# Last units, expert layer and linear attention: another order of the tensor engine and seven rotating banks

## The reference

```python
attn = jax.nn.softmax(jnp.einsum('bgnc,bgckn->bgnk', qf, ks_), axis=-1)
out = jnp.einsum('bgnk,bgckn->bgnc', attn, vs_)          # layer 1: the value sums
...
router_probs = jax.nn.softmax(x @ router_w + router_b, axis=-1)
top_p, top_i = jax.lax.top_k(router_probs, K)
top_p = top_p / jnp.sum(top_p, axis=-1, keepdims=True)
expert_out = jnp.einsum('bnd,edc->bnec', x, expert_w) + expert_b
gathered = jnp.take_along_axis(expert_out, top_i[..., None], axis=2)
return jnp.einsum('bnk,bnkc->bnc', top_p, gathered)      # layer 4: the experts
...
q = (x @ wq_w.T + wq_b).reshape(b, s, h, d)              # layer 5: k and v likewise
q = jax.nn.elu(q) + 1.0
k = jax.nn.elu(k) + 1.0
kv_cos = jnp.einsum('bshx,bshz->bhxz', k_cos, v)
qkv = jnp.einsum('bshx,bhxz->bshz', q_cos, kv_cos) + jnp.einsum('bshx,bhxz->bshz', q_sin, kv_sin)
denom = 1.0 / (... + 1e-05)
```

## Time and profile before

| | us |
|---|---|
| median of 3 runs | 216.42 (215.61 to 217.93) |
| profiled execution | 216.58 |
| its span, first to last instruction | 214.8 |

### The profile page before, as it was taken

One profiled execution on the slowest core, in us unless ns is written; L12 is line 12 of the kernel. 1 busy time (PEld: TensorE's weight loads), 2 busy tenths in 40 slices (PEclk: granted clock), 3 DMA queues, 4 the chain that ended last, 5 costly groups with the idle time before them and its releaser, 6 DMA issues.

```text
span 214.8 us, 6817 instructions
## 1 busy us (share of the span) xinstructions
PE 186.6 (87%) x2969; PEld 136.4 (64%) x2969; DVE 154.1 (72%) x347; ACT 97.3 (45%) x239; POOL 39.2 (18%) x57
## 2 busy tenths in 40 slices
PE   7999989899997989974898798598499969979994
PEld 2677668899997889721344684244147737735993
DVE  2789997958999999869777166595768749646101
ACT  3734997478888778511003350200868510035100
POOL 4970000012421440540100301133000000110000
PEclk9999999999999999999699999969955999999999
DMA  6830426345455510000143140001200190000000
GB/s 180 285 117 5 154 95 201 107 133 197 150 158 166 180 49 3 4 0 5 22 159 99 27 110 0 0 5 32 67 25 3 25 366 22 0 0 0 3 0 24
DMA packets 9042, 17.07 MB, mean 79 GB/s; under 512 B 2504, under 2 KB 3752, under 8 KB 8884
## 3 DMA queue, kind: packets, MB, share of 16 engines
q1 hardware_dynamic: 8868, 16.34, 24.1%
q10 hardware_dynamic: 144, 0.30, 0.4%
HBM read 16.20 MB, written 0.42 MB: 77 GB/s over the span
## 4 chain that ended last, share of the span: by engine, by line
PE 57%; DVE 26%; issue 6%; ACT 5%; POOL 2%; DMA 2%; POOLq 1%; DVEq 0%
PE ps L1540 55%; DVE onehot L1068 5%; POOL rstd L578 2%; DVE dots L1094 2%; DMA cst<-in_cst 2%; DVE arena L453 2%; DVE att L1118 1%; ACT arena L641 1%; DVE stu_fq L1443 1%; ACT onehot L837 1%; ACT table L641 1%; ACT arena L858 1%; DVE dots L1100 1%; DVE arena L1524 1%; DVE arena L1048 1%
## 5 line engine op out<-in xcount | busy, mean ns | idle before, releaser
L1540 PE MATMUL ps<-table,onehot 128*128 128x64 bf16 x1728 | 52.9, 194 | 5.0 <-issue 2.8
L1540 PEld LDWEIGHTS ps<-table,onehot 128*128 128x128 bf16 x1728 | 51.5, 98 | 6.5 <-issue 4.8
L1540 PE MATMUL ps<-spare 128*128 128x512 bf16 (+1 forms) x128 | 36.6, 419 | 8.1 <-DVE rexp L1359 2.3
L725 ACT ACTIVATE arena<-ps 128x512 f32<-128x512 f32 (+1 forms) x40 | 21.5, 553 | 14.2 <-PE ps L1540 13.9
L1540 PEld LDWEIGHTS ps<-spare 128*128 128x128 bf16 x128 | 12.4, 109 | 24.4 <-issue 6.8
L453 POOL TENSOR_TENSOR arena<-arena,w4p 128x288 f32<-128x288 f32 x21 | 16.2, 803 | 57.9 <-DVE arena L453 57.8
L1540 PE MATMUL ps<-arena 128*32 128x66 f32 (+4 forms) x388 | 25.2, 281 | 0.2 <-DVE arena L1320 0.2
L1540 PEld LDWEIGHTS ps<-arena 128*32 128x32 f32 (+2 forms) x388 | 22.2, 156 | 4.1 <-issue 1.4
L578 POOL TENSOR_TENSOR rstd<-var_eps,cst 128x4 f32<-128x4 f32 (+2 forms) x9 | 8.8, 982 | 82.7 <-DVE var_eps L937 56.1
L641 ACT ACTIVATE arena<-ps 128x512 f32<-128x512 f32 (+3 forms) x16 | 7.0, 469 | 26.1 <-PE ps L1540 20.3
L1068 DVE TENSOR_SCALAR onehot<-indexb,cst 128x2304 bf16<-128x2304 bf16 (+1 forms) x24 | 17.7, 771 | 0.0
(11 more groups left out here) (280 smaller groups left out, 305.0 us busy)
## 6 DMA issues: line engine op xcount, KB each, us to landing
indexb<-index_rows SPq DMA_DIRECT2D x20, 288.0 KB, 3.3
stu_fq<-index_rows SPq DMA_DIRECT2D x8, 288.0 KB, 3.4
arena<-in_toep SPq DMA_DIRECT2D x1, 2120.5 KB, 9.6
l<-in_l SPq DMA_DIRECT2D x1, 646.5 KB
stu_fq<-in_stu SPq DMA_DIRECT2D x1, 560.0 KB, 3.8
onehot<-in_l3w SPq DMA_DIRECT2D x1, 512.0 KB
table<-stu_mixed SPq DMA_DIRECT2D x4, 128.0 KB, 2.2
l<-in_l SPq DMA_DIRECT2D x1, 384.0 KB, 7.3
```

The source lines that it names most:

```text
L725: nc.scalar.activation(gv[:, b % 2, :, at:at + count, :], ps[:, SB[n % len(SB)], 0:count * SLOT].rearrange("p (s a d) -> p a s d", s=count ...
L1540: return nc.tensor.matmul(out_ap, lhsT, rhs, start=start, stop=stop)
```

## The change

1. The sum over corners of unit 6 (`L - 1`) moves from VectorE to TensorE, like that of unit 5; the two have banks of their own. On VectorE the sum of unit 5 comes later, behind the logits of unit 7. The six spares around "linear middle" and "linear low" go; "linear low" and two spares now stand between the two transpositions of the heads.
2. Two spares instead of four in the attention.
3. In the expert layer five spares instead of eight behind the moments; the first half's expert products are ahead of the second half's transposition; the four spares behind the weighing go.
4. Linear attention: keys and values rotate over seven banks (2t mod 7, 2t + 1 mod 7), bank 7 is for transpositions and spares. The second half's transposition stands ahead of the first value products; from value tile 3 on, each step waits for one `vs`, and issues a value tile, the next key tile and a spare. Queries, key-value products and denominators take other banks.

The diff, cut; the lines that only rename banks on the reading engines are left out:

```diff
-        KBANK, VBANK = (lambda t: 2 * t % 8), (lambda t: (2 * t + 1) % 8)
+        SLOTS, FREE = 7, 7
+        KBANK, VBANK = (lambda t: 2 * t % SLOTS), (lambda t: (2 * t + 1) % SLOTS)
+        QB, KVB, DEN, DSUM = (FREE, 2, 3, 4), (5, 6, 0, 1), 5, 6
-        corner_sums = ps[:, 4, 0:J * HC]
+        corner_sums = lambda u: ps[:, 4 + u % 2, 0:J * HC]
...
-                if t == 3:
-                    rows_copied(t5, a5, 1, VBANK(0))
+                if t == 0:
+                    rows_copied(t5, a5, 1, FREE)
...
-                values_from_corners(L - 2)
                 weighted_dots(L)
...
                 nv.reciprocal(pinv[:, 0:own], psum_[:, 0:own]).then_inc(v1.sem, v1.step("inv0"))
+                values_from_corners(L - 2)
                 weights(L)
...
-                dve.wait_ge(s_pv, L)
-                dve.wait_ge(v1.sem, v1[f"part{L - 1}"])
-                value_sums(L - 1)
+                values_from_corners(L - 1)
...
             corners_of(L - 2)
+            pe.wait_ge(s_pv, T - 1)
+            pe.wait_ge(v1.sem, v1[f"part{L - 1}"])
+            corners_of(L - 1)
             weights_prepared("linear middle")
-            occupied_after(v1, ("inv0", 3), bank=6)
-            weights_prepared("linear low")
-            occupied_after(v1, (f"mixed{L - 1}", 3), bank=6)
             for h in range(NH):
+                if h == 1:
+                    weights_prepared("linear low")
+                    occupied(2, 6)
                 pe.wait_ge(v1.sem, v1[f"att{h}"])
...
-            occupied(4, 0)
+            occupied(2, 0)
             pe.wait_ge(a3.sem, a3["vt"])
...
-            occupied_after(v4, ("var0", 4), ("eps1", 4), bank=6)
+            occupied_after(v4, ("var0", 5), bank=6)
             turned_rows(v4, t4, 0, 4)
-            occupied(1, 6)
-            turned_rows(v4, t4, 1, 5)
             pe.wait_ge(d_moe, 5 * 16)
             for h in range(NH):
+                if h == 1:
+                    turned_rows(v4, t4, 1, 5)
                 pe.wait_ge(a4.sem, a4[f"rows{h}"])
...
-            occupied_after(v4, ("rlog1", 4), ("rank1", 4), ("esel", 4), ("gated", 4), bank=4)
+            occupied_after(v4, ("rlog1", 4), ("rank1", 4), ("esel", 4), bank=4)
...
+            pe.wait_ge(v4.sem, v4["gated"])
             tile_biases(range(B), KBANK, WK, stop=False)
-            occupied_after(v4, ("x41", 3), bank=7)
-            tile_biases(range(B - 1), VBANK, WV, stop=False)
-            occupied_after(v5, ("cen1", 3), bank=7)
-            turned_rows(v5, t5, 0, 7)
+            tile_biases(range(B - 2), VBANK, WV, stop=False)
+            pe.wait_ge(v4.sem, v4["ynorm1"])
+            tile_biases([B - 2], VBANK, WV, stop=False)
+            occupied(2, FREE)
+            turned_rows(v5, t5, 0, FREE)
             pe.wait_ge(a5.sem, a5["rows0"])
             tile_products("k", range(B), KBANK, WK, start=False)
-            tile_biases([B - 1], VBANK, WV, stop=False)
-            tile_products("v", range(B), VBANK, WV, start=False)
-            pe.wait_ge(v5.sem, v5["vs0"])
-            turned_rows(v5, t5, 1, VBANK(0))
-            for pair in ((4, 5), (6, 7)):
-                for name, bank, w, freed in (("k", KBANK, WK, "fk"), ("v", VBANK, WV, "vs")):
-                    pe.wait_ge(v5.sem, v5[f"{freed}{pair[1] - 4}"])
-                    if name == "v" and pair[0] == 4:
-                        pe.wait_ge(a5.sem, a5["rows1"])
-                    tile_biases(pair, bank, w, stop=False)
-                    pe.wait_ge(a5.sem, a5["rows1"])
-                    tile_products(name, pair, bank, w, start=False)
+            turned_rows(v5, t5, 1, FREE)
+            tile_products("v", range(B - 1), VBANK, WV, start=False)
+            pe.wait_ge(a5.sem, a5["rows1"])
+            occupied(3, FREE)
+            for t, freed in ((B - 1, "vs0"), (B, "vs1"), (B + 1, "vs2"), (B + 2, "vs3")):
+                pe.wait_ge(v5.sem, v5[freed])
+                tile_biases([t], VBANK, WV, stop=False)
+                tile_biases([t + 1], KBANK, WK, stop=False)
+                tile_products("v", [t], VBANK, WV, start=False)
+                tile_products("k", [t + 1], KBANK, WK, start=False)
+                occupied(1, FREE)
+            pe.wait_ge(v5.sem, v5["fk4"])
+            tile_biases([T - 1], VBANK, WV, stop=False)
+            tile_products("v", [T - 1], VBANK, WV, start=False)
...
-                            pe.wait_ge(v5.sem, v5[f"fq{b}" if pair else f"vs{B + b // 2}"])
-                        mm(ps[:, b, at], lin_w[rows, w], ln_rows[rows, :], stop=False)
+                        if g == 0 and (pair or b):
+                            pe.wait_ge(v5.sem, v5[f"fq{b}" if pair else ("vs4", "fk5", "vs5")[b - 1]])
+                        mm(ps[:, QB[b], at], lin_w[rows, w], ln_rows[rows, :], stop=False)
...
             queries(0)
+            occupied_after(v5, ("fk6", 4), bank=KVB[0])
             pe.wait_ge(v5.sem, v5[f"vs{T - 1}"])
             keys_values(0)
```

35 lines of the change are left out of this document (17 added, 18 removed).

## The result

The changed kernel takes 213.19 us (median of 19 executions, 211.39 to 221.70) against 215.97 us (19 executions, 213.76 to 217.93) for the kernel before: ratio 0.989 [0.986, 0.992], a gain of 1.1% (1.3% by the medians) where 2.4% was forecast. The profiled execution takes 212.75 us (span 211.0) against 216.58.

A forecast was written before the change was run, and what follows sets the result against it. The prediction took the chain through TensorE at half clock, with VectorE setting the pace or waiting, as the bound. Seven terms summed to -5.45 us, from 216.58 or the median 216.42 to a stated 211.2; 8-in-10 range 209.8 to 214.4.

The forecast's parts named there:

- A: Last units: unit 6's sum on TensorE keeps the clock at full for the projection; -0.55 us.
- B: Expert layer: first half's products go ahead of the second transposition, so the first logits come earlier; -0.75 us.
- D: Start of the linear attention: first transposition no longer starts late, with two spares left of six; -0.9 us.
- E: Linear attention: second transposition ahead of the value products delays the first value tile; +0.75 us.
- F: Linear attention tiles: with seven banks the steps fit and VectorE runs at 1.26 us a tile; -1.85 us.
- G: Queries and key-value products: third key-value group 4.0 us after VectorE's last value tile, where it was 4.74; -0.75 us.
- C: Expert sum: twelve spares at full clock end VectorE's 1.38 us wait; -1.4 us, with 0.7 back at half clock.
- one short stretch: Rival: clock falls once for 3.4 us, near the expert sum or first keys and values; 213.0 us, chance 0.22.
- From there on the order is the old one.: Behind the third key-value group's start: order as before, so no further gain or loss counted; 0 us.
- first rival: Linear attention: clock falls before the first keys and stays at half through the tiles; 219.2 us, chance 0.10.
- Waits come back elsewhere: Rival, linear attention: steps of 1.9 us even at full clock and late queries; 213.8 us, chance 0.06.
- no change: Rival: half clock merely moves from the tiles to the denominators' expansion after 170 us; 215.5 to 217 us, chance 0.07.

The follow-up runs named there:

- lower group: Executions of the unaltered changed kernel at the lower times: 14 of the first 19, within 211.4 and 214.6 us.
- upper group: Executions of the unaltered changed kernel near 221 us: five of the first 19, at 220.7 to 221.7 us, mean granted clock 0.93 to 0.94.

## Why the prediction was too large, and what of it held

The direction and the range held, and in the profiled execution six of the seven terms, within 0.15 us of the forecast: A (-0.44), B, D, E, F and G. The seven banks do what the working said, step by step. That the eighth value tile stands at 159.12 (forecast 159.1) and the third key-value group at 163.91 (163.8) is luck: the forecast's times leave A's 0.55 out, and the 0.73 by which everything came earlier there makes up for what C and E fell short. The gain of the profiled execution is 3.8 us for 5.45, and that of the medians 2.8 for 5.2. Three steps failed, and a fourth, term A, came out for another reason than the one given.

**Term C, "VectorE reaches its wait at 144.6 ... so the 1.38 us go".** The prediction had the price of the other case beside it (0.7 comes back at half clock) and took the full clock. The trace has 0.54 there and 0.52 us came back. The changed kernel's two traces show full clock once and half clock once, and where it is at full here it is at half at the first keys, which costs 1.2. So the failed step is the size of C: -1.4 forecast, -0.87 measured, and the clock is the reason. The sum left out a stretch that sits in both of these traces, at one place or the other; of the 16 traces other than that of the kernel before eleven have one at the expert sum, three at the first keys and two neither. It was the rival *one short stretch* (213.0, chance 0.22) which describes the profiled execution, with 212.75, and it deserved the largest chance.

**"From there on the order is the old one."** This put all that follows the key-value products at nothing. The order was the old one, the time was not: +0.97 in the denominators, TensorE waiting for "issue". In the kernel before the first two key-value groups ran at half clock (3.47 us), and no pause followed, nor in the traces of the old rotation, of the steps without spares and of the old last units, where they ran at half clock too. Where they take 2.05, the pause is 0.26 to 1.53 us or, in the two executions with spares behind the queries, none of note, and L1477 stands 4.28 to 5.40 us behind the query tiles, against 4.29. The forecast counted on the full clock's 2.05 in place of 3.47 in term G and did not ask whether what follows keeps up. At full clock the same place costs nothing in one execution (4.29) and 1.1 in another, so the missing term is a spread and not a price. Shown is that the Toeplitz transfer is not the cause and that the pause has no fixed length; that it is the supply of instructions was argued and is not shown. The cause of the 0.97 stays open.

**The first rival's chance, 0.10.** Its mechanism was right (step of 2.79 us for 2.65, clock at 0.50 through the tiles), its time of 219.2 low for 220.7 to 222.9: in the one trace of this order it starts at the first keys and lasts past the queries, to 172. It takes place in 15 of 44 executions. The prediction treated the clock as a property of the order, one case or another for the whole kernel. It differs from execution to execution, so a chance of one third should have gone into the median too: 14 executions alone have 212.75, all 19 have 213.19, 0.44 more. The argument against the rival was "full-width spares now stand in every step". Without them the time is 216.17 and no mean clock is above 0.960, so they matter; but with them the clock fell in the tiles near 155.1 in one trace, of a kernel with the same linear attention, and when it had fallen ahead of them TensorE was busy 3.00 of 3.00 us with those spares and the clock did not come back for over 20 us.

**Term A, "so I expect the clock to stay at full for the projection: half of its 1.19 us at half clock, -0.55".** The -0.44 is right for that pair of traces, and it is the clock's and not the order's. Of the 14 traces with the new last units twelve have a stretch at half clock at 94 to 101, at the corner sums; only the profiled execution and one other have none. It costs nothing while the corner sums run (4.27 us at either clock) and up to 0.8 where it reaches the weights' products behind them: VectorE's step comes 40.87 to 41.66 us behind the first corner sums. The old order has 41.31 and 41.40 with the projection at half clock and 40.68 with it at full. So at full clock the new last units are 0.19 us slower, and that undoing them shows 212.59 against 212.72 fits.

The kernel before is a draw as well, which neither the prediction nor the terms take in. Its 86 executions beside the experiments lie at 213.4 to 215.3 us where the mean clock is above 0.965 (25 of them, median 214.2), at 215.0 to 218.4 between 0.95 and 0.965 (38), and at 217.6 to 219.5 below (23). The profiled execution with 216.58 us and 0.96 is of the middle. Against the 25 the lower group of the changed kernel, 212.72, gains 1.5 us (on several chips): that much is left where the clock is high in both, about half of the 2.8 between the medians.

The Trainium skill ("TensorE: Matmul & The Clock Gate", A second HAM failure mode: psum-queue depth-cycling) puts such a fall down to short pauses from cycling through the banks. The trace of the old last units, with a fall within the steps and TensorE busy 3.20 of 4.00 us from 152 to 156, agrees with it. But a third of the executions of the changed kernel fall, and none of 38 with spares or the value products moved to the first keys, all with the same rotation, so the rotation alone does not decide here.

*Waits come back elsewhere* and *no change* fell: steps are 1.50 us, and no half-clock stretch lies in 164 to 180 in the traces of the lower group.

The best versions have the second transposition behind the value products: 211.41 to 211.86 us in 24 executions of four kernels, none above 214.1, 1.7 to 2.5% under the kernel before by their ratios and some 1 us under the lower group of the changed kernel. They cannot be told from one another. That the upper group is gone is shown for them together (none of 24, where 15 of 44 would give 8), not for each.

## What to carry to other kernels

Where an engine's clock may fall, forecast a distribution: list the thin places, say what a fall costs at each, and expect that each execution draws one of them. That holds for the kernel one starts from as well: compare executions of like mean clock before a term is read from one pair of traces. Spare products are a bet. In these runs they made a fall rarer (3 at the first keys: none of 12 executions near 221, from a third; 7 in the steps: 212.7 in two thirds of the executions, for 216.2), they did not bring back a clock that was down, and a step with one then took 2.79 us. So they belong ahead of the first place where a fall would last. And parts of a change that meet in one resource need not add: the last units and experts alone showed no gain (216.17 against 216.5), the linear attention alone had 8 of 12 executions above 220, and together they gave a ratio of 0.989.
